# One core, a two-layer decoder block: the levels of the delta stage's triangular inverse work on half of each head's columns

## The reference, cut to what matters

```python
def step(S, x):
    q_t, k_t, v_t, b_t, g_t = x
    S = S * jnp.exp(g_t)[..., None, None]
    for i in range(NH):                       # NH = 2 updates for each token
        ki, vi, bi = (k_t[:, i], v_t[:, i], b_t[:, i])
        kv = jnp.einsum('bhk,bhkv->bhv', ki, S)
        S = S + bi[..., None, None] * jnp.einsum('bhk,bhv->bhkv', ki, vi - kv)
    o_t = jnp.einsum('bhk,bhkv->bhv', q_t, S)
    return (S, o_t)
...
_, o = jax.lax.scan(jax.checkpoint(step), S0, xs)   # 1024 tokens, batch 2, 4 heads, keys of 128, values of 64
```

## Time and profile before

| | us |
|---|---|
| median of 3 runs | 2616.49 (2614.86 to 2620.75) |
| the profiled execution's own time | 2616.09 |
| its span | 2614.3 |
| granted TensorE clock, mean over the span | 0.941 of full speed |
| busy over the span: PE, PEld, DVE, ACT, POOL | 2287.6, 1873.6, 1641.1, 1163.2, 735.1 |

### The profile page before, as it was taken

How to read it: one execution, slowest core, us unless ns; L and a number is a source line. 1 busy time by engine, 2 the same in 40 slices (tenths; PEclk the granted TensorE clock), 3 DMA queues, 4 the chain that set the end, 5 groups by cost and what they waited for, 6 DMA issues and landing times. The chain is left out here.

```text
span 2614.3 us, 62054 instructions
## 1 busy us (share of the span) xinstructions
PE 2287.6 (88%) x25731; PEld 1873.6 (72%) x25731; DVE 1641.1 (63%) x3593; ACT 1163.2 (44%) x3232; POOL 735.1 (28%) x876
## 2 busy tenths in 40 slices
PE   5689989999898999964998589988887799999998
PEld 4477777777785777743887366666665688888887
DVE  4566676667644555546784455556775767767776
ACT  2544444443423554521554356656775233333332
POOL 2334243423323333331565433420011001111110
PEclk8699999999999999976999799999998899999999
DMA  3101010100103000020442300000000000000000
GB/s 100 57 10 35 27 35 10 35 27 13 61 3 108 9 18 13 13 82 17 114 124 34 103 2 2 2 2 2 2 2 14 13 25 25 25 25 25 25 7 33
DMA packets 87961, 83.35 MB, mean 32 GB/s; under 512 B 27264, under 2 KB 83456, under 8 KB 86272
## 3 DMA queue, kind: packets, MB, share of 16 engines
q1 hardware_dynamic: 81536, 70.98, 8.7%
q0 software_dynamic: 6144, 8.39, 1.9%
HBM read 68.71 MB, written 10.65 MB: 30 GB/s over the span
## 5 line engine op out<-in xcount | busy, mean ns | idle before, releaser
L2566 PE MATMUL bank<-f_XH,f_wp 128*128 128x512 f32 x1088 | 365.4, 397 | 5.9 <-issue 4.5
L782 DVE SCALAR_TENSOR_TENSOR a_acc<-a_praw,a_convw,a_acc 128x256 f32<-128x256 f32 x345 | 205.4, 596 | 99.4 <-ACT a_acc L930 91.2
L2566 PEld LDWEIGHTS bank<-f_XH,f_wp 128*128 128x128 f32 x1088 | 209.1, 192 | 48.5 <-issue 4.9
L2566 PEld LDWEIGHTS bank<-f_wp,f_Hp 128*128 128x128 f32 x1632 | 215.0, 192 | 28.6 <-DVE X L2703 17.0
L2566 PE MATMUL bank<-f_wp,f_Hp 128*128 128x256 f32 x1632 | 219.3, 284 | 17.2 <-DVE X L2703 16.3
L2566 PE MATMUL bank<-f_XL,f_wp 128*128 128x512 f32 x544 | 216.6, 398 | 0.0
L2701 DVE SCALAR_TENSOR_TENSOR X<-bank,f_w,X 128x256 f32<-128x256 f32 x512 | 211.4, 476 | 0.0
L2750 POOL TENSOR_TENSOR f_wp<-wa,f_wp 128x768 fp32r<-128x768 f32 x34 | 62.8, 1848 | 526.2 <-ACT f_wp L2716 526.2
L2739 ACT ACTIVATE f_Hp<-f_H 128x512 fp32r<-128x512 f32 x136 | 85.9, 632 | 225.9 <-DVE f_H L2688 225.9
L582 PE MATMUL bank<-XT,wa 128*128 128x256 f32 x512 | 160.5, 446 | 7.6 <-ACT a_acc L930 6.6
L2737 ACT ACTIVATE f_G<-bank 128x512 f32<-128x512 f32 x136 | 81.3, 598 | 166.0 <-PE bank L2566 166.0
(11 more groups left out here) (370 smaller groups left out, 5439.2 us busy)
## 6 DMA issues: line engine op xcount, KB each, us to landing
wa<-in_c_w SPq DMA_DIRECT2D x64, 256.0 KB, 3.3
wa<-in_f_gu SPq DMA_DIRECT2D x34, 256.0 KB, 2.8
wb<-grown SPq DMA_DIRECT2D x4, 1536.0 KB, 6.8
a_KQg<-grown SPq DMA_DIRECT2D x4, 1536.0 KB, 6.6
wa<-in_f_d SPq DMA_DIRECT2D x34, 128.0 KB, 2.9
a_E<-decays SPq DMA_DIRECT2D x16, 256.0 KB, 4.0
X<-in_x SPq DMA_DIRECT2D x4, 512.0 KB, 5.3
wa<-in_a_wqkv SPq DMA_DIRECT2D x1, 2048.0 KB, 11.9
```

What stands on the lines that cost most here:

```text
L782: i = v.e.scalar_tensor_tensor(A_, praw[:, c, :, j:j + BT_], convw[:, c, j:j + 1], A_, ALU.mult, ALU.add)
L2566: i = t.e.matmul(out_, lhsT[x], rhs[y], start=n == 0 and k == 0, stop=n == 2 and k == nk - 1, skip_group_check=True)
```

## The change

In every level the products are formed for those 32 columns of each head only that the level's mask can select, the columns of the moving operand being picked with a stride; the bank then holds them side by side (`packed`, 4 x 32 columns for one product). ScalarE copies 128 instead of 256 columns from the bank, into the strided columns of `y_`. VectorE copies under the mask with 128 instead of 256 columns, and where one instruction served both X and its transpose (512 columns) there are now two of 128. The stationary operands are as before, 64 columns wide. The other columns of `y_` are never written by a first use, so GpSimd clears both `y_` tiles at the start. Order, buffers, banks and semaphores stay.

```diff
+            cols = lambda x, l, w: x.rearrange("p (n w s) -> p n w s", w=2, s=LEVELS[l])[:, :, w, :]
+            of_heads = lambda x, l, w: x.rearrange("p h (n w s) -> p h n w s", w=2, s=LEVELS[l])[:, :, :, w, :]
+            mask = lambda l, w: cols(masks[:, l, w, :], l, w).unsqueeze(1).broadcast_to([P, H, R // 2 // LEVELS[l], LEVELS[l]])
+            packed = lambda ap, l, w=0: ap[:, w * H * R // 2:(w + 1) * H * R // 2].rearrange("p (h n s) -> p h n s", h=H, s=LEVELS[l])
...
 # "xi", TensorE
-                                i = t.e.matmul(heads(b.ap)[both(bb), h, :], nt[c % 2][both(bb), h, :], block[both(bb), :],
+                                i = t.e.matmul(packed(b.ap, 0)[both(bb), h], nt[c % 2][both(bb), h, :], cols(block, 0, 0)[both(bb)],
...
 # "Y", TensorE
-                                i = t.e.matmul(heads(b.ap)[both(bb), h, :], nt[c % 2][both(bb), h, :], xx[c % 2][both(bb), 0, h, :],
+                                i = t.e.matmul(packed(b.ap, l)[both(bb), h], nt[c % 2][both(bb), h, :],
+                                               cols(xx[c % 2][:, 0, h, :], l, 0)[both(bb)],
...
 # "X", TensorE
-                                    t.e.matmul(heads(b.ap)[both(bb), h, :], xt[both(bb), h, :], y[both(bb), h, :],
+                                    t.e.matmul(packed(b.ap, l)[both(bb), h], xt[both(bb), h, :], cols(y[:, h, :], l, 0)[both(bb)],
...
-                                i = t.e.matmul(heads(b.ap[:, H * R:])[both(bb), h, :], y[both(bb), h, :], xt[both(bb), h, :],
+                                i = t.e.matmul(packed(b.ap, l, 1)[both(bb), h], y[both(bb), h, :], cols(xt[:, h, :], l, 1)[both(bb)],
...
 # "xi", VectorE
-                        v.e.copy_predicated(xx[c % 2][:, 1], mask(1), nt[c % 2])
+                        v.e.copy_predicated(of_heads(xx[c % 2][:, 1], 0, 1), mask(0, 1), of_heads(nt[c % 2], 0, 1))
                         filled(v, *s)
-                        v.e.copy_predicated(xx[c % 2][:, 0], mask(0), heads(b.ap)).then_inc(b.emptied, 1)
+                        v.e.copy_predicated(of_heads(xx[c % 2][:, 0], 0, 0), mask(0, 0), packed(b.ap, 0)).then_inc(b.emptied, 1)
 # "X", VectorE
-                            i = v.e.copy_predicated(xx[c % 2], masks[:, l].unsqueeze(2).broadcast_to([P, 2, H, R]),
-                                                    b.ap.rearrange("p (w h r) -> p w h r", w=2, h=H))
-                        else:
-                            i = v.e.copy_predicated(xx[c % 2][:, 1], masks[:, l, 1, :].unsqueeze(1).broadcast_to([P, H, R]),
-                                                    heads(b.ap[:, H * R:]))
-                        i.then_inc(b.emptied, 1)
+                            v.e.copy_predicated(of_heads(xx[c % 2][:, 0], l, 0), mask(l, 0), packed(b.ap, l))
+                        v.e.copy_predicated(of_heads(xx[c % 2][:, 1], l, 1), mask(l, 1), packed(b.ap, l, 1)).then_inc(b.emptied, 1)
 # "Y", ScalarE
-                        c.e.activation(y_[ch % 2], heads(b.ap), ACT.Copy).then_inc(b.emptied, 1)
+                        c.e.activation(of_heads(y_[ch % 2], l, 0), packed(b.ap, l), ACT.Copy).then_inc(b.emptied, 1)
 # GpSimd, at the start
+                for y in y_:
+                    g_.e.memset(y, 0.0)
```

More of the change, by code:

```diff
@@ L861, in vector @@
                         c = s[1]
-                        mask = lambda w: masks[:, 0, w, :].unsqueeze(1).broadcast_to([P, H, R])
                         v.wait_ge(x_start.sem, x_start.at[c,])
-                        v.e.copy_predicated(xx[c % 2][:, 1], mask(1), nt[c % 2])
+                        v.e.copy_predicated(of_heads(xx[c % 2][:, 1], 0, 1), mask(0, 1), of_heads(nt[c % 2], 0, 1))
                         filled(v, *s)
-                        v.e.copy_predicated(xx[c % 2][:, 0], mask(0), heads(b.ap)).then_inc(b.emptied, 1)
+                        v.e.copy_predicated(of_heads(xx[c % 2][:, 0], 0, 0), mask(0, 0), packed(b.ap, 0)).then_inc(b.emptied, 1)
                     elif what == "X":
```

## The result

The changed kernel takes 2742.2 us (median of 4 runs, 2730.05 to 2749.38) against 2616.65 for the kernel before; the ratio is 1.047, 95% interval 1.043 to 1.051. It is 125 us slower. The profiled execution took 2738.82 us, span 2737.0, 122.7 more than the span before.

A forecast was written before the change was run, and what follows sets the result against it. TensorE's own work was taken to bound stage A (busy 90%), its waits second. Base 2616 plus 95 us (24.4 against 21.3 us a chunk, 31 times, copies' gain included, matmuls 0) gave 2711 us, range 2625 to 2795.

The forecast's parts named there:

- Pace of the matmuls: Stage A's 15 changed matmul groups a chunk: stationary loads set their pace, so halved columns save 0 (bounds 0 to 3.5 us).
- The clock: TensorE in stage A: clock falls about as before but returns much later, lower-level share 0.12 to 0.50, +3.1 us a chunk.
- the middle between two extremes: Share 0.50 of stage A at the lower clock, between a clock that behaves as now and one that doesn't return.
- falls of 40 us: Stage A: at share 0.50 each stretch at the lower clock lasts about 40 us, against 6 before.
- the formula: Stage A's chunk period: full-clock 19.6 us and lower-clock 32.4 us mixed by time share; 24.4 us at share 0.50.
- 31 times: Stage A's 31 chunk periods between first and 32nd level 0, each 3.1 us longer: +95 us.
- the prediction's list by s: Stage A's chunk period by lower-clock share s: 20.6 us at 0.12, 21.2 at 0.20, 22.6 at 0.35, 24.4 at 0.50.
- the prologue's narrow matmuls: 128 gapless prologue records of 12 moving columns, 7.01 us, loads 227 ns: read as not bringing the clock back.
- the rule of the Trainium skill: TensorE kept busy without gaps keeps its clock up; supports the rival of a clock as before, 2594 us, chance 0.15.
- The copies: VectorE's and ScalarE's narrower copies in stage A shorten TensorE's waits: 22 us or 0.7 a chunk, between 10.7 and 52.
- Twice the direct part: Copies' gain in stage A: 10.7 us direct, doubled to 22 because one or two instructions usually precede an awaited copy.
- The memsets: Two clears ahead of GpSimd's first normalisation step, hidden in 4.49 us of idle time: 0, at most 0.5 us.

## Why the prediction was right

*Pace of the matmuls.* Booked at 0, measured near 0: at full clock groups start 0.47 us apart inside the stream, as before, and 0.49 instead of 0.51 at its head. That the stationary side sets the pace was argued then from L648 and L651; the run with 32 stationary columns shows it.

*The clock.* The step that carried the forecast held: the clock falls about as often as before (17 times against 15) and comes back much later. Stretches at 0.50 of tens of us appeared, and the mean clock was forecast 0.75 and came out 0.74. That the share hit so closely (0.52 for 0.50) is in good part luck. No row gave 0.50; it was the middle between two extremes. Its picture of falls of 40 us, with as much full-clock time between them as before, did not come out either: they last about 24 us, and the time between them shrank from 38 to 22 us. The periods had been put at 19.6 and 32.4 us at the two levels; the two chunks read above, each at one level alone, took 18.3 and 33.7. With the share measured, 0.52, the formula gives 1 / (0.48 / 19.6 + 0.52 / 32.4) = 24.7; measured 24.9. (With 18.3 and 33.7 it would give 24.0: a chunk that holds one of the long waits is longer than these two.) The forecast of +95 was short of +125 by two things: 0.5 us a chunk, of which the share is 0.3, in all 15 us, and the scans of the last chunks behind the 32nd level 0, 11 us, which "31 times" left out. Two entries of the prediction's list by s are 0.1 low (its formula gives 21.3 for 0.20 and 22.7 for 0.35), which changes nothing.

One reading behind this step is weaker than it was put. That the prologue's narrow matmuls ran at the lower level was taken from their durations; the granted clock of the same profile reads 1.00 there, and shows no change before about 41 us. The load times speak for the prediction: at 98 us, where the clock reads 0.50, loads of the same shape take up to 228 ns, as the 227 of L594. So the two sources differ, and what carries the step now are the runs in stage A.

```profile
27.00:34.00 7.00, 6.89 (x128) 1.00 0.01 2
98.00:99.50 1.50, 1.50 (x25) 0.50 0.00 0
...
L651 PEld LDWEIGHTS bank<-wb x256: 133/138/228, 98.4 to 689.2; 128*64 128x64 f32 x128
```

By the rule of the Trainium skill weighed there (TensorE: Matmul & The Clock Gate, section "Why this matters for your kernels": keep TensorE continuously busy), read as records without gaps, the clock should have stayed up. The stretch from 170 to 230 us speaks against that reading: 60.00 of 60.00 us busy, clock 0.50. What the runs show beside it is that with 16, 32, 48 and 64 moving columns in the same slots the mean clock is 0.68, 0.76, 0.87 and 0.94.

*The copies.* This term of the sum was mis-sized: 22 us forecast, 5 measured (2 to 9 by the interval), below its own lower bound of 10.7. With 64-column matmuls the waits of the earlier trace rows fell by 4 us only, from 63.7 to 59.5. Two things stand behind it.

First, the work. VectorE's busy time for the same work, first to last level 0, fell by 22 us (436.06 to 413.83) and not by 35. How much sooner an awaited copy ends depends on the level. Two copies in a row overlap, so from level 2 on the pair takes 0.48 us from the first start to the second end (339.56 to 340.04) where one copy had taken 0.73. In level 1, where the picked columns stand in runs of two, the pair takes 0.73 (177.21 to 177.94): nothing is saved. In level 0, with runs of one, L871 of the new kernels takes 0.49 where the whole-head copy had taken 0.43, and the 17 waits that end on it grew from 13.6 to 15.1 us.

```profile
101.50:761.60 660.10, 436.06 (x882) 0.94 0.08 25
102.80:757.10 654.30, 413.83 (x1005) 0.94 0.08 25
...
PE bank L675 <- DVE wa L877: 28.8, 16, 2.9
PE bank L675 <- DVE wa L871: 15.1, 17, 2.6
PE bank L685 <- ACT wa L998: 13.2, 8, 1.8
PE bank L689 <- ACT wa L998: 2.4, 5, 0.8
...
339.56 0.28 DVE L876 COPY_PREDICATED wa<-masks,bank 128x128 f32<-128x128 uint8 x1
339.76 0.28 DVE L877 COPY_PREDICATED wa<-masks,bank 128x128 f32<-128x128 uint8 x1
...
177.21 0.45 DVE L876 COPY_PREDICATED wa<-masks,bank 128x128 f32<-128x128 uint8 x1 [1.91 <-PE bank L689]
177.45 0.49 DVE L877 COPY_PREDICATED wa<-masks,bank 128x128 f32<-128x128 uint8 x1
```

The first line is the kernel before, the last two the changed kernel, all others the one with 64-column matmuls and narrow copies.

Second, TensorE's long waits are not made of copies. VectorE before the awaited L871 at 340.46, in the kernel before:

```profile
337.75 1.15 DVE L782 SCALAR_TENSOR_TENSOR a_acc<-a_praw,a_convw,a_acc 128x256 f32<-128x256 f32 x1
338.82 0.24 DVE L831 RECIPROCAL a_cn<-a_kss 128x16 f32<-128x16 f32 x1
...
340.46 0.72 DVE L871 COPY_PREDICATED wa<-masks,bank 128x512 f32<-128x512 uint8 x1
```

Between L782 and the copy stand the eight short instructions of the step "small" (L831 is its first) and one of L898. Behind them TensorE waited 2.73 us; with narrow copies and 64-column matmuls the same wait was 2.63:

```profile
340.10 0.68 PE L675 MATMUL bank<-wa 64*64 64x64 f32 x16 [2.63 <-DVE wa L877]
```

"Twice the direct part" assumed that the instructions ahead of a releaser were copies too.

*The memsets* cost nothing that the span shows, and behind stage A nothing moved, as booked.

The size of the falls is not explained in full: why the share flattens at 16 columns was not looked into, and why the changed kernel's runs spread over 19 us (2730 to 2749) is left open.

## What to carry to other kernels

Before columns are cut from a matmul, look at whether its moving columns or its stationary load sets the distance between starts; if it is the load, the cut saves nothing, and cutting the stationary side is what pays. Then look at the granted clock of the stretch: taking columns out of a stream that keeps its pace can hold TensorE at 1.2 GHz for tens of us in a stage that was at 2.4, and added columns that cost no time can bring it back. A copy that is halved by picking columns gains only if the picked columns stand in runs (here of four or more), and only where that copy, not what is queued ahead of it, is what is waited for.

## What the runs showed that was not expected

- Doubling the streamed columns of 480 groups (15 a chunk) makes a kernel that is 133 us faster than the changed one, at no cost in pace.
- VectorE's masked copy of 128 columns took 0.28 to 0.30 us with picked columns in runs of 4 to 32, 0.44 to 0.49 in runs of 1 and 2, whether they came from a packed bank or from their places.
- A kernel with 32 columns on both sides, which leaves out half of the rows, was 55 us faster than before, though its clock was 0.87 and TensorE waited longer.
